# Two kinds of store leave SP's queue: the cached weight slabs to POOL's, the output tiles to ACT's

## The reference

```python
def _layernorm(x, axis=-1, eps=1e-5):
    m = jnp.mean(x, axis=axis, keepdims=True)
    v = jnp.var(x, axis=axis, keepdims=True)
    return (x - m) / jnp.sqrt(v + eps)

# data (2, 8192, 4096) f32; both weights (4096, 4096) f32; mask (4096, 4096) int32
# attn: block_mask = mask.reshape(128, 32, 128, 32).sum(axis=(1, 3)) > 0, spread to elements
#       out = einsum('bsk,nk->bsn', data, weight * elem_mask)
# ffn:  out = einsum('bsi,oi->bso', x, sign(weight)) + bias
x = x + _layernorm(attn(_layernorm(x), weight, mask))
x = x + _layernorm(ffn(_layernorm(x), weight2, bias))
```

## Time and profile before

| | us |
|---|---|
| median of 2 runs | 3410.71 (3403.91 and 3417.51) |
| the profiled execution | 3412.63 |
| span of its slowest core (core 5) | 3411.1 |
| spans of the other cores | 3365.5 to 3402.4 |

### The profile page before, as it was taken

How to read it: one execution, slowest core, us unless ns; L and a number is a source line. 1 busy time by engine, 2 the same in 40 slices (tenths; PEclk the granted TensorE clock), 3 DMA queues, 4 the chain that set the end, 5 groups by cost and what they waited for, 6 DMA issues and landing times.

```text
span 3411.1 us, 24248 instructions; the slowest of 8 cores (3365.5 to 3411.1 us)
## 1 busy us (share of the span) xinstructions
PE 2026.9 (59%) x9272; PEld 933.1 (27%) x9272; DVE 884.6 (26%) x1300; ACT 606.0 (18%) x460; POOL 343.9 (10%) x296
## 2 busy tenths in 40 slices
PE   1013133444315545555894799579669966965992
PEld 0011011112112212222342344334234432433441
DVE  0043534333420010124013222410222142022214
ACT  0120000000163333332114200201340030115000
POOL 3555554100000000000000000000000000000000
PEclk9997676677657777777897899889789977987996
DMA  3467676557336666663643354363324435332442
GB/s 124 130 243 246 206 253 214 181 189 230 130 110 208 199 208 197 205 214 142 205 155 115 119 178 148 123 222 148 123 105 160 180 124 222 148 123 74 151 158 111
DMA packets 72947, 573.15 MB, mean 168 GB/s; under 512 B 8800, under 2 KB 8816, under 8 KB 42112
## 3 DMA queue, kind: packets, MB, share of 16 engines
q1 hardware_dynamic: 58752, 444.62, 37.6%
q0 software_dynamic: 14080, 126.97, 11.2%
HBM read 470.86 MB, written 100.70 MB: 168 GB/s over the span
## 4 chain that ended last, share of the span: by engine, by line
PE 40%; DMA 31%; DVE 11%; ACT 11%; issue 4%; POOL 1%; SPq 0%; DVEq 0%; ACTq 0%; POOLq 0%
PE pmm L476 39%; DMA WST<-w1s 12%; DMA WST<-w2s 11%; DVE WSL L395 4%; DMA out<-OS 3%; ACT WSL L409 2%; DMA XS<-x 2%; ACT HS L766 2%; ACT HS L735 2%; DVE OS L814 2%; ACT HT L215 1%; DMA WSL<-c1m 1%; DVE BNST L595 1%; DMA OS<-mask 1%; PE ptA L205 1%
## 5 line engine op out<-in xcount | busy, mean ns | idle before, releaser
L476 PE MATMUL pmm<-WSL,HT 128*128 128x512 bf16 x8192 | 1899.0, 396 | 820.6 <-ACT WSL L409 248.7
L476 PEld LDWEIGHTS pmm<-WSL,HT 128*128 128x128 bf16 x8192 | 825.4, 101 | 1885.0 <-issue 1003.8
L532 DVE TENSOR_TENSOR ARAW<-pmm,BIASF 128x512 bf16<-128x512 f32 x128 | 88.5, 692 | 1006.2 <-PE pmm L476 1006.2
L395 DVE TENSOR_TENSOR WSL<-WST,BTE 128x1024 bf16<-128x1024 f32 x128 | 228.4, 1799 | 322.3 <-DMA WST<-w1s 309.8
L205 PE MATMUL ptA<-IDN,HS 128*128 128x128 bf16 x576 | 64.7, 302 | 363.7 <-ACT HS L766 236.7
L513 DVE BATCH_NORM_STATS2 BNST<-ARAW 128x6 f32<-128x512 bf16 x96 | 59.3, 680 | 544.2 <-ACT ARAW L503 544.2
L409 ACT ACTIVATE WSL<-WST 128x1024 bf16<-128x1024 f32 x128 | 133.4, 1054 | 186.5 <-DMA WST<-w2s 186.3
L205 PEld LDWEIGHTS ptA<-IDN,HS 128*128 128x128 bf16 x576 | 56.6, 139 | 377.1 <-issue 376.3
L259 POOL TENSOR_TENSOR XP<-XP 128x2048 int32<-128x2048 int32 (+4 forms) x80 | 131.3, 1641 | 120.5 <-DMA XP<-mask 112.5
L564 POOL DMA_DIRECT2D XS<-x x24 | 13.3, 555 | 1143.0 <-ACT HS L629 1075.7
L215 ACT ACTIVATE HT<-ptA 128x2048 bf16<-128x2048 bf16 x36 | 67.6, 1877 | 274.0 <-PE ptA L205 274.0
(11 more groups left out here) (59 smaller groups left out, 746.7 us busy)
## 6 DMA issues: line engine op xcount, KB each, us to landing
WSL<-c1m SPq DMA_DIRECT2D x48, 2048.0 KB, 8.6
WSL<-c2m SPq DMA_DIRECT2D x48, 2048.0 KB, 8.1
WST<-w1s SPq DMA_DIRECT2D x128, 512.0 KB, 5.8
WST<-w2s SPq DMA_DIRECT2D x128, 512.0 KB, 4.6
XS<-x POOLq DMA_DIRECT2D x48, 1024.0 KB, 5.7
OS<-mask POOLq DMA_DIRECT2D x16, 2048.0 KB, 9.7
XP<-mask POOLq DMA_DIRECT2D x16, 2048.0 KB, 10.7
c1m<-WSL SPq DMA_DIRECT2D x16, 2048.0 KB, 7.9
```

The source lines that it names most:

```text
L395: ins = v.tensor_tensor(dst, src, mk, op=OP.mult)
L476: ins = t.matmul(acc_bank(use8, nsl, tt), st_ap, mv_ap, start=(kh == 0 and j == 0), stop=(kh == 1 and j == KTS - 1))
L532: ins = v.tensor_tensor(dst, acc_bank(use8, nsl, tt), BIASF[:, nsl * 512:(nsl + 1) * 512], op=OP.add)
```

## The change

The store of a finished slab in chunk 0 is issued by POOL, no longer by SP, with the same wait and the same semaphore; it stands at the same place of the program, which puts it among POOL's fronts and tails. The store of an output tile is issued by ACT, no longer by SP, with the same wait. Nothing else is touched.

```diff
@@ emit_w_load_prep, chunk 0 @@
-                @blk.sync
-                def _(s):
-                    wt(s, ready)
+                @blk.gpsimd
+                def _(g):
+                    wt(g, ready)
                     sn = "sC%d" % (su % 2)
-                    s.dma_start(cm_d[layer][sl, :, :], buf[:, :]
+                    g.dma_start(cm_d[layer][sl, :, :], buf[:, :]
                                 ).then_inc(sem[sn], 16)
@@ emit_finalize_tile @@
-            @blk.sync
+            @blk.scalar
             def _(s, tt=tt):
                 wt(s, fin[tt])
                 s.dma_start(out_d[t0 + tt * 128: t0 + (tt + 1) * 128, :],
```

## The result

| | before | changed |
|---|---|---|
| median, us | 3417.7 (10 runs) | 3322.8 (11 runs) |
| profiled execution, us | 3412.6 | 3315.9 |
| spans of the 8 cores, us | 3365.5 to 3411.1 | 3289.8 to 3314.3 |

The ratio is 0.9734, with a 95% interval of 0.971 to 0.9758: 2.7% faster. The forecast was 3301 us and a gain of 3.2%; the time lies in its range. In the profile after, the queues show the move: the stores are no longer among what SP issued. The columns are packets, MB and the share of the 16 engines' time.

What follows compares the result with a forecast made beforehand. Bound: in chunk 0 the loop of 512 KB weight loads, in chunks 1 to 3 PE's matmuls. Terms 58 + 20 + 10 + 22 = 110 us off 3412.6 gave 3302.6, about 3301 against the median; range 3235 to 3375.

Steps and rivals of the forecast that it cites:

- Part 1: Layer 1 of chunk 0, slab stores on POOL: a slab takes 27.3 us, 3.9 less; 15 save 58 us.
- Part 2: Layer 0 of chunk 0 after the mask fronts: slabs 10, 12, 13, 14 and 15 gain 3.9 us each, 20 us.
- Part 3: Layer 0 beside POOL's mask fronts: the move adds waits, stalls missed by 3 and 11 us; 10 us gained.
- The waits named: Layer 0, POOL's order: store 1 goes out only behind front 4; front 5 can't start before slab 2 is ready.
- Part 4: Output stores on ACT, chunks 1 to 3: slab 3's load leaves earlier; 22 us saved, ends 0 and 36.
- A: Rival: the store is hidden altogether, 23.8 us a slab; 182 us saved, 3230 us; chance 0.2.
- B: Rival: the store only moves, its bytes delay loads as before, only issue time is saved; 3377 us; chance 0.13.
- C: Rival: POOL becomes a chain beside mask fronts, fronts 4 to 7 take 118 us each; about 3472 us; chance 0.05.
- D: Output stores wait on ACT, late evacuations cost more: -15 in place of 22, about 3340 us; counted with the forecast.

## Why the prediction was right, and where it was off

**Part 1, layer 1: right, by two errors that cancel.** A slab was forecast at 27.3 us and takes 27.4; 58 us were forecast and 51.7 came on the mean core, because the forecast was set against the slowest core's 31.18 while the mean core had 30.9, and because slab 10 takes 31.9 us: the two x loads for the next chunk, which the forecast had as covered, share its time. The two terms were both off. The loop without the store's bytes was put at 23.8 + 0.6 = 24.4 and measured 23.1. The bytes were put at 2.9 and measured 4.3. That is the upper end I had (4.4, from loads beside mask loads). The working under it was wrong: it had the two loads in flight hit for 1.5 and 4.4 us and took their mean. Measured, the older one pays nothing, the one issued with the store 2.3 us and the next one 1.6, and these add up. Without slab 10 a slab takes 27.1 us.

**Part 2, late layer 0: right, in part by luck.** 17.6 us for 20. The odd slabs kept 38.2 to 38.6 us, as forecast. But 3.9 us were forecast for each of five slabs, and slabs 10, 13, 14 and 15 gained 2.1 to 3.3; slab 12 gained 7.2, because two loads of x left it for a place where they cost nothing. The forecast had no such term. The two kernels with late stores on SP leave these loads where they were, and there slab 12 gains 2 us and the stage 12.3. The gap ahead of even slabs, put at about 6 us, is 2.0 and 2.3.

**Part 3, beside the fronts: this step failed, with a small sum.** +10 was forecast, -3.9 measured, inside the ends of -30 to +25. The waits named were real, their effect was another. "What waits for an odd store is the first multiply two slabs on" was the wrong place to look: the gap ahead of odd slabs stayed 18.4 to 18.7 us on the mean core, and no multiply waited for a store. The cost came through the fronts: front 7 started 22.5 us later than before (552.3 for 529.8), and slab 7, whose multiplies (590.8 to 611.9) had met only its last 7 us, took 66.9 us in place of 39.9. The even slabs did gain, by 10.4 us each on the mean of slabs 2, 4, 6 and 8, and the odd ones gave 45 us back over the four. I had costed what the fronts do to the stores, but not what it costs a slab to have a front moved onto it. The run with layer 0's stores out of POOL's order shows this as the cause: 16.6 us come back, which is 12.8 under before and close to the +10. The runs with them on ACT and with all of them late on SP, whose front 7 starts at 528.9 and 523.8, give 12.9 and 18.6 back. How much is front and how much slab is best read in pairs: slabs 6 and 7 take 94.2 us together before, 100.7 changed, 90.2 and 91.4 in the runs with late stores on SP and on ACT.

**Part 4, output stores on ACT: right.** 24 us for 22: 6.0, 8.7 and 9.3 us by chunk. The store left 4.7 us earlier, rounds took 14.4 us on the mean (14.7 forecast), and PE's one wait for ACT was 25.5 us (25 forecast).

**The rivals.** A fell with the 64 KB stores: 23.1 us would have been the slab if the bytes were hidden. B fell with the run of layer 1's stores alone. The Trainium skill (DMA: Bandwidth & Descriptors, Issuing engines are not separate DMA queues) states that transfers of all issuers run on the same 16 engines, so that another issuer saves only the time of issuing. The runs agree as far as the other queue by itself goes: late stores on SP and stores on POOL take 27.2 and 27.4 us a slab. But the saving of 3.5 us a slab wasn't the time of issuing (0.33 us); it was the loads that no longer stood behind a wait. C's waits were there, but fronts 4 to 7 took 68.5 to 71.6 us on the mean core (67.4 to 70.4 before), not 118: POOL's order cost about 17 us and not 160. D did not come.

**The sum.** 90 us measured on the mean core and 95 between the medians, 110 forecast. The 20 that are missing on the mean core are 14 from part 3, 6 from part 1, 2 from part 2, less 2 from part 4. The absolute time missed by 21.8 us; 7.0 of it is that before's median over 10 runs is 3417.7 and not the 3410.7 of the two runs shown.

## What to carry to other kernels

In an engine's queue, look at what could already go but stands behind a waiting store: putting the store behind the next loads in the same queue was worth as much as moving it to another engine, and it put no wait into another engine's order. When a wait is moved into another engine's order, ask not only who waits for the moved instruction, but what that engine's own long work will run beside once it starts later. Free room on the DMA engines does not make a transfer free: with 64 KB stores they were busy for 0.63 to 0.65 of their time (1100 to 1300 us, eight cores), and the full store cost 4.3 us a slab. The nearest rows of the same trace (loads beside mask loads, 4.4 us longer) were closer to that price than the weighted 2.9, in this one case. And list what else stands behind the moved instruction: by the same move the loads of x left one slab (about 5 us) and came into another (about 5 us).

## What the runs showed of the hardware that was not expected

- A 2 MB store beside the 512 KB loads cost the loop 4.3 us of the store's landing time of 7 to 10, from POOL's queue and from SP's alike (27.4 and 27.2 us a slab), and 3.9 us in rows of 4 KB (27.0 for 23.1). The size of its rows mattered by 0.5 us at most.
- Stores from POOL land later than the same stores did from SP ahead of the loads: 10.2 and 10.4 us at the median in the two layers, against 7.9 and 7.2 before. It is the company and not the queue: stores issued by SP behind two loads land in 12.6 and 10.8 us. In the changed kernel nothing waited for them.
- DVE's multiply slows down only while POOL adds. Before and in the changed kernel, each multiply that ran while a front was on but beside none of its additions took 1.22 to 1.23 us (149 in each, 8 cores), mask loads or not; those with additions beside them for over 90% of their time took 2.9 and 3.1 us at the median. With nearly all bytes of the mask loads of fronts 4 to 7 gone it is 3.1 still. In slab 7, the worst, the mean is 3.6 us.
- The same 240 GB/s took 0.71 of the engines' time with the slab in one store and 0.84 with it in eight pieces.
